# TensorE warmed on zeros before x arrives, the router's sums in one product, and a table fill in 128-byte rows

## What is computed

```python
xn = _layernorm(x, axis=-1)
s = _L0_attn_ref(xn, ...)        # q, k, v; context = phi_q * cumsum(phi_k * v) * SCALE; @ Wo + bo
g = _silu(_L0_ffn_ref(xn, ...))  # each token's logits = xn @ router_w.T, top 2 of 8 experts,
                                 # 256 slots an expert, gelu(buf @ w1.T + b1) @ w2.T + b2
x = x + s * g
```

## Time and profile before

| What | Value |
|---|---|
| Median of 3 runs | 2004.76 us (2004.38 to 2006.69) |
| The profiled execution | 2003.46 us, its span 2001.3 us |
| PE busy | 1971.3 us, 99% of the span |
| DVE, ACT, POOL busy | 69%, 35%, 26% |
| HBM read and written | 268.51 MB and 163.10 MB |

### The profile page before, as it was taken

The page is one execution under the profiler, slowest core; times in us unless marked ns, Lnnn a source line. Parts: engine busy times, 40 slices in busy tenths (PEclk is TensorE's granted clock), DMA queues, the critical chain, the costliest instruction groups (busy, mean ns, idle before and its releaser), DMA issues.

```text
span 2001.3 us, 27188 instructions
## 1 busy us (share of the span) xinstructions
PE 1971.3 (99%) x9396; PEld 904.9 (45%) x9396; DVE 1385.0 (69%) x2099; ACT 707.6 (35%) x1112; POOL 511.3 (26%) x640
## 2 busy tenths in 40 slices
PE   8999999999999999999999999999999999999996
PEld 2355555555444444444444444444444444444442
DVE  3788788888877777776777797564455565456656
ACT  1442222222754345344335443522212322222322
POOL 0038888888302311321310010110000000000002
PEclk9999999999999999999999999999999999999998
DMA  9546667666899888977877879673333233334535
GB/s 353 215 148 226 215 224 232 233 232 201 295 338 281 260 245 265 276 238 273 263 257 238 292 249 328 203 222 103 102 102 100 93 112 99 116 106 157 184 113 129
DMA packets 182219, 416.26 MB, mean 208 GB/s; under 512 B 18592, under 2 KB 71392, under 8 KB 179680
## 3 DMA queue, kind: packets, MB, share of 16 engines
q1 hardware_dynamic: 138736, 284.26, 42.7%
q0 software_dynamic: 34912, 121.71, 19.9%
q10 hardware_dynamic: 8464, 8.92, 1.4%
HBM read 268.51 MB, written 163.10 MB: 216 GB/s over the span
## 4 chain that ended last, share of the span: by engine, by line
PE 91%; DVE 3%; DMA 2%; issue 1%; ACT 1%; POOL 0%; SPq 0%; ACTq 0%; DVEq 0%; POOLq 0%
PE pair L2132 36%; PE pair L2103 32%; PE pair L1942 18%; PE pair L1892 2%; PE pair L1971 2%; DMA spare<-up_sums 1%; PE pair L1993 1%; DMA arena<-x_t 1%; DMA routing<-kvs_dram 0%; PE pair L1905 0%; DVE arena L1653 0%; DMA arena<-up_sums 0%; PE pair L2072 0%; DVE arena L1313 0%; ACT arena L1033 0%
## 5 line engine op out<-in xcount | busy, mean ns | idle before, releaser
L2132 PE MATMUL pair<-arena 128*128 128x512 f16 x3360 | 730.2, 379 | 1.6 <-DVE arena L1678 0.5
L2103 PE MATMUL pair<-xnT,arena 128*128 128x512 f16 x2400 | 525.4, 379 | 2.0 <-ACT xnT L1040 1.9
L2132 PEld LDWEIGHTS pair<-arena 128*128 128x128 f16 x3360 | 327.8, 98 | 400.7 <-issue 7.7
L1678 DVE SCALAR_TENSOR_TENSOR arena<-pair,arena 128x1024 f32<-128x1024 f32 x234 | 286.1, 1223 | 150.6 <-PE pair L2132 149.7
L1942 PE MATMUL pair<-arena 128*128 128x512 f16 x1728 | 382.6, 379 | 0.8 <-ACT xnT L911 0.8
L1114 ACT ACTIVATE arena<-arena 128x512 f16<-128x512 f32 x280 | 171.9, 628 | 555.6 <-PE pair L2132 500.7
L2103 PEld LDWEIGHTS pair<-xnT,arena 128*128 128x128 f16 x2400 | 234.3, 98 | 286.6 <-ACT xnT L1040 3.7
L1942 PEld LDWEIGHTS pair<-arena 128*128 128x128 f16 x1728 | 168.8, 98 | 192.6 <-ACT xnT L911 1.2
L2103 PE MATMUL pair<-xnT 128*128 128x512 f16 x960 | 213.7, 379 | 0.0
L1653 DVE SCALAR_TENSOR_TENSOR arena<-arena 128x512 f16<-128x512 f32 x280 | 189.6, 689 | 16.5 <-ACT arena L1114 15.8
L835 POOL DMA_DIRECT2D s_dram<-arena x8 | 6.2, 778 | 596.4 <-DVE arena L1678 596.4
(11 more groups left out here) (213 smaller groups left out, 1836.8 us busy)
## 6 DMA issues: line engine op xcount, KB each, us to landing
down_dram<-arena SPq DMA_DIRECT2D x70, 512.0 KB, 6.6
arena<-down_dram SPq DMA_DIRECT2D x70, 512.0 KB, 3.3
up_dram<-arena SPq DMA_DIRECT2D x90, 256.0 KB, 6.1
arena<-up_dram SPq DMA_DIRECT2D x90, 256.0 KB, 2.6
arena<-down_sums SPq DMA_DIRECT2D x40, 512.0 KB, 6.1
arena<-w_up POOLq DMA_DIRECT2D x36, 512.0 KB, 5.3
up_sums<-arena POOLq DMA_DIRECT2D x36, 512.0 KB, 3.7
arena<-up_sums SPq DMA_DIRECT2D x66, 256.0 KB
```

Of the source, the lines that this page charges most:

```text
L1678: ins = nc.vector.scalar_tensor_tensor(to, src, scale, to, ALU.mult, ALU.add)
L2103: ins = mm(out_to, w[:, a, c * P:(c + 1) * P], x_in_op[:, b, c, :], start=(first and i == 0), stop=(i == 11), skip_group_check=True)
L2132: ins = mm(down_banks(j, t // 2)[:, (t % 2) * BLOCK:(t % 2 + 1) * BLOCK], g_ops[:, A_NAMES.index(DOWN_A[j]), c, a, t * P:(t + 1) * P], dow ...
```

## The change

1. PE no longer starts with the router's sums. It multiplies zeros, `nothing`, a stretch of the arena that DVE sets to zero in its first instruction, in 11 f16 products of 512 columns into a bank that nobody reads. Then it scores block 0 as soon as the router, the ninth column (`pool_consts` 1) and x are there. It waits no longer for `const_ready`.
2. DVE adds up the router's weights over the chunks (`tensor_reduce` into `rw_chunks`, 128 x 8), so that one product with `ones_f` is enough. It stands between the halves of block 0.
3. POOL sets the ninth column and `ones_f` first, each with a signal of its own.
4. The fill of `meta_dram` is written as "(p t) c": each partition writes 16 slots in a row, 128 bytes, where it wrote 16 pieces of 8 bytes that lie 1024 bytes apart. As every slot gets the same pair, the table holds the same.
5. `zeros_ready` counts DVE's three signals (zeros, sums over chunks, `ident_f`); `ident_ready` is gone.

```diff
+        nothing = part(16, 1)[:, 0:BLOCK // 2]
+        rw_chunks = table(N4, "p (e o) -> p e o", e=EXPERTS, o=1)
...
             ch = Chain(pool, pool_consts)
+            ch.step(nc.gpsimd.memset(rw_f[:, :, EXPERTS:EXPERTS + 1], 1.0))
+            ch.step(nc.gpsimd.memset(ones_f, 1.0))
             nc.gpsimd.memset(ones[:, :], 1.0)
-            nc.gpsimd.memset(ones_f, 1.0)
-            nc.gpsimd.memset(rw_f[:, :, EXPERTS:EXPERTS + 1], 1.0)
...
-            pool.dma_start(meta_dram.rearrange("(t p) c -> p t c", p=P), meta_s[:, :, :]).then_inc(meta_filled, 16)
+            pool.dma_start(meta_dram.rearrange("(p t) c -> p t c", p=P), meta_s[:, :, :]).then_inc(meta_filled, 16)
...
+            nc.vector.memset(nothing, 0.0).then_inc(zeros_ready, 1)
...
+            dve.wait_ge(router_loaded, 16)
+            nc.vector.tensor_reduce(rw_chunks[:, :, :], rw_f[:, :, 0:EXPERTS].rearrange("p c e -> p e c"),
+                                    AX.X, ALU.add).then_inc(zeros_ready, 1)
             dve.wait_ge(const_ready, 1)
             nc.vector.tensor_copy(iota[:, :], iota_i)
-            nc.vector.tensor_copy(ident_f, ident[:, 0:EXPERTS + 1]).then_inc(ident_ready, 1)
+            nc.vector.tensor_copy(ident_f, ident[:, 0:EXPERTS + 1]).then_inc(zeros_ready, 1)
...
-            pe.wait_ge(const_ready, 1)
-            pe.wait_ge(router_loaded, 16)
-            for c in range(CH):
-                ins = mm(bank[3][:, 0:EXPERTS], ones_f, rw_f[:, c, 0:EXPERTS], start=(c == 0), stop=(c == CH - 1))
-            ins.then_inc(sums_w_done, 1)
-            pe.wait_ge(ident_ready, 1)
...
+            pe.wait_ge(zeros_ready, 1)
+            zeros = nothing.bitcast(F16)
+            for _ in range(11):
+                mm(out_bank(2), zeros[:, 0:P], zeros, start=True, stop=True)
+            pe.wait_ge(router_loaded, 16)
+            pe.wait_ge(pool_consts, 1)
             pe.wait_ge(xt_first, 16)
             scores_by_expert(0, range(CH // 4))
             pe.wait_ge(xt_loaded[0], 16)
             scores_by_expert(0, range(CH // 4, CH // 2)).then_inc(xt_half, 1)
+            pe.wait_ge(pool_consts, 2)
+            pe.wait_ge(zeros_ready, 2)
+            mm(bank[3][:, 0:EXPERTS], ones_f, rw_chunks[:, :, 0], start=True, stop=True).then_inc(sums_w_done, 1)
             second_half(0, 1, range(CH // 2, CH)).then_inc(scores_done, 1)
+            pe.wait_ge(zeros_ready, 3)
```

More of the change, by code:

```diff
@@ L293, in out_bank @@
             return bank[i // 2][:, (i % 2) * BLOCK:(i % 2 + 1) * BLOCK]
-        sums_w_done = sem("sums_w_done")
-        const_ready, ident_ready = sem("const_ready"), sem("ident_ready")
+        zeros_ready, sums_w_done = sem("zeros_ready"), sem("sums_w_done")
+        const_ready = sem("const_ready")
         router_loaded, biases_loaded = sem("router_loaded"), sem("biases_loaded")
```

## The result

The changed kernel takes 2000.2 us (median of 11 runs, 1999.52 to 2001.17), the kernel before in the same group 2005.12 us (2003.54 to 2006.69): 4.9 us less, a ratio of 0.9976 with a 95% interval of 0.9966 to 0.9985. The profiled execution takes 2000.25 us with a span of 1998.0, 3.3 us less than the span before. By the interval, the gain in the medians lies between 3.0 and 6.8 us.

A forecast was written before the change was run, and what follows sets the result against it. PE, busy 99% of the span, bounds the kernel, so only an earlier start gains. Block 2 at 21.3 to 21.5 instead of 25.66 us gives 4.2: 2004.76 - 4.2 = 2000.6 us, forecast 2000.2 to 2001.2, range 1999.2 to 2003.0.

The forecast's parts named there:

- Two dates that do not add: Block 2 starts at the later of DMA and PE dates: fill alone 1.5 us, PE's part alone nothing, together 4.2.
- the stall: Start-up loads: block 1's first half takes 7.1 us where it needs 2.5, 4.6 us that every later load inherits.
- The DMA date: Landing of block 2's first half of x: 21.3 us with the new fill, against 25.6 before.
- The 0.3 us that I left of it: Remainder of the loads' 4.6 us hold-up if it goes by pieces, 16 times fewer: 4.6/16 = 0.3 us.
- The PE date: When PE can start block 2 after zeros, block 0 and block 1: 21.05 to 22.5 us, in the middle 21.5.
- a late clock: Cost at block 0 if PE's full clock comes after scoring begins: nothing at 5.0, 0.45 us at 6.8, 1.45 at 8.6.
- The clock: PE's rise from 1.2 to 2.4 GHz during start-up, with zeros from 1.3 us: expected between 5.0 and 8.6 us.
- The rival of zeros that don't count as activity: PE's clock rises as late as 11.6, block 2 at 23.9, gain down to 1.7 us; late-clock rival's chance 0.17.
- No give-back: Behind 98 us nothing but the shift: no later stretch gives back what the start won.
- The median: Whole kernel: median of the runs shown, 2004.76, less 4.2 gives 2000.6 us.

The follow-up runs named there:

- pe_only: The changed kernel with the old fill (2048 pieces of 8 bytes): median 2005.52 us, ratio 1.0007 to the kernel before.
- fill_late: The changed kernel with POOL issuing the fill only when all of w_kv is split, near 80 us: median 2000.17 us.
- fill_32: The changed kernel with the fill in 512 pieces of 32 bytes: one run, 2001.1 us against 2005.22 before.
- router_rows: The changed kernel with the router loaded in 128 pieces of 256 bytes into its own tile, then copied by DVE: median 1999.69 us.
- no_zeros: The changed kernel without the eleven products of zeros: median 2002.59 us.
- fill_only: The kernel before with the new fill alone (128 pieces of 128 bytes): median 2003.16 us, ratio 0.9996.
- zeros_6: The changed kernel with 6 products of zeros instead of 11: one run, 2004.84 us against 2005.22 before.
- rows_and_late: The changed kernel with both the router loaded in whole rows and copied by DVE, and the fill issued near 80 us: median 1999.36 us.
- fill_16: The changed kernel with the fill in 1024 pieces of 16 bytes: one run, 2002.46 us against 2005.22 before.
- sums_first: The changed kernel with the router's sums as eight products again, between the zeros and block 0: median 2000.20 us.

## Why the prediction was right, point by point

- **Two dates that do not add.** Shown. Without the stall but with PE's old start 1.4 us, with PE's new start but the stall nothing, together 4.1 by the dates. The prediction had 1.5, 0 and 4.2. The nothing of pe_only has another make-up than forecast: x came at 25.2, not at 25.6, and PE's wait cost it 1.6 us by the clock, which the prediction did not foresee.
- **The DMA date.** The stall was the fill's and went with it, as forecast. The 0.3 us that I left of it do not exist (fill_late, fill_32). In place of it the second half of block 0 landed 0.5 us later than in the profile of before, which is spread, and block 2's x landed at 21.5 against a forecast of 21.3.
- **The PE date.** Zeros from 1.26 (1.3 forecast) to 5.6, scores from 5.6 (5.8 to 6.1), the sums' product 0.39 us (0.2 to 0.45), hidden behind x. No new wait was late: DVE's sum stands at 3.96 and takes 0.27. From the second half of block 0 on, the rest went as summed: that half began at 10.2, and 3.45 + 7.95 us behind it block 2 starts, at 21.57. The forecast of 21.5 was made up otherwise, from x at 9.65 and 0.45 us for a late clock. The clock rose at 5.05 us and cost nothing, and x came 0.5 us late. These two misses cancel, so that the date was met to 0.1 us is in part luck; the mechanism is not.
- **The clock.** Forecast between 5.0 and 8.6 us. A trace's record of the granted clock begins with this rise, and the stretches print 1.00 for the time ahead of it, though the spacing of the loads there is that of the half clock. By this record, with eleven zeros it rose between 4.8 and 7.2 us in the nine profiled executions that have them, which cost between nothing and 0.5 us (in router_rows). The rival of zeros that don't count as activity is refuted by no_zeros, where it rose at 11.0. That rival had priced such a rise about right: block 2 at 23.9 for a rise at 11.6, measured 23.56. What was mis-sized is the expectation of no_zeros, which had the clock rise 3.7 us after the scores began; it took 5.4 there, and 3.0 in fill_only.
- **No give-back.** Partly open. By the dates the two profiled executions differ by 4.08 us at 71 us, by 3.3 at the end, and the medians of 11 runs by 4.9. Over the other kernels the span is between 3.6 us less ahead than the date at 71 us (zeros_6) and 0.3 us more (router_rows, rows_and_late). The profiled execution of before was one of its fastest (2003.46, its runs 2003.54 to 2006.69), which makes most of the others look as if they had lost. The steps sit at waits for DVE and ACT, and they come also where no lead was won (pe_only), so they are no sign of a give-back. That the start gives back nothing at all is not shown.
- **The median.** The forecast of 2000.6 took before's median of 3 runs, 2004.76. With the 11 runs of the same group it is 2005.12, and the gain 4.9 us in place of 4.2. The interval (3.0 to 6.8) holds both.

## What to carry to other kernels

A start-up has two clocks to race, the loads' and the engine's, and an edit to one is worth what the other leaves of it: work out both dates before costing either, and test each edit alone. A constant table that is written in 8-byte pieces can hold up a full load queue by a hundred times what its bytes are worth (4.2 to 4.6 us, against 0.04 for 16 KB at 418 GB/s); if the pattern is the same in each row, write it in the order of the partitions. Dummy products raise the clock before the data comes, but let them last until the data is there: in the one run with six of the eleven they were worth nothing. And a wait that is left behind them can lose the clock again, as in pe_only.

## What the runs showed of the hardware that was not expected

- **Tiny writes.** 2048 writes of 8 bytes beside full loads from HBM held up the loads by 4.2 to 4.6 us, 1024 of 16 bytes by 1.4, 512 of 32 bytes by 0.1, and 128 of 128 bytes by nothing (the middle two in one run each). The Trainium skill (DMA: Bandwidth & Descriptors, Specifications) puts the border at 512 bytes; here writes of 32 and 128 bytes, far below it, held up a full load queue by 0.1 us at most. Whether the writes themselves ran at full rate is not shown.
- **One wait lowers the clock.** A wait of 3.58 us (pe_only) brought the granted clock to 0.50 for some 3.4 us of dense products, at a cost of about 1.6 us. In fill_16, which waits 1.08 and 1.85 us for x, the loads stay 0.43 us apart.
- **Products of zeros count as work.** f16 products of zeros raised the clock at 4.8 to 7.2 us; the same kernel without them had it at 11.0 (no_zeros), and the two with the old start, where products of 8 columns ran from 4.42 us and of 512 columns from 8.0, at 11.0 and 11.6 (fill_only, before).
- **Small f32 products follow the clock.** Sixteen matmuls of 8 columns with their 128 x 128 f32 weights take 2.03 us at full clock (sums_first) and 3.5 at half.
